# Bias folds and denominators of a fused graph layer, moved into four column tiles of 32

## The reference, cut to what matters

```python
xn = layernorm(x)
# graph part: a second layernorm with gain and bias, then attention over edges
x2 = layernorm(xn) * ln_g + ln_b
q, k, v = x2 @ Wq + bq, x2 @ Wk + bk, x2 @ Wv + bv
# softmax over the edges of a node of (q . k) * scale * edge weight, times v
gnn = xn + (values @ W1 + b1) @ W2 + b2
# mixer: linear attention
Q, K, V = elu(xn @ mWq + mbq) + 1, elu(xn @ mWk + mbk) + 1, xn @ mWv + mbv
kv = einsum('shd,she->hde', K, V)
z  = 1 / einsum('shd,hd->sh', Q, K.sum(0))        # the denominators
mix = einsum('shd,hde,sh->she', Q, kv, z) @ mWp + mbp
x = x + gnn + mix
x = x + ffn(layernorm(x))                          # digits of a one-hot code, elementwise
```

## Time and profile before

| what | value |
|---|---|
| median of three runs | 835.73 us |
| time of the profiled execution | 838.25 us |
| its span, first to last instruction | 836.1 us |
| mean granted TensorE clock | 0.974 |
| PE busy | 771.1 us, 92% |
| DVE, ACT, POOL busy | 67%, 43%, 47% |
| share of PE in the chain that ended last | 85% |

### The profile page before, as it was taken

One profiled execution on the slowest core, in us unless ns is written; L12 is line 12 of the kernel. 1 busy time (PEld: TensorE's weight loads), 2 busy tenths in 40 slices (PEclk: granted clock), 3 DMA queues, 4 the chain that ended last, 5 costly groups with the idle time before them and its releaser, 6 DMA issues.

```text
span 836.1 us, 13681 instructions
## 1 busy us (share of the span) xinstructions
PE 771.1 (92%) x4752; PEld 468.5 (56%) x4791; DVE 562.4 (67%) x1293; ACT 358.0 (43%) x834; POOL 393.0 (47%) x391
## 2 busy tenths in 40 slices
PE   1999998989999999969999999999999999999964
PEld 1564445544456444426666666666666876776742
DVE  4478584964232513358888888988888786786874
ACT  0321301022302122026666666666666764565562
POOL 1017787777777777777777777640000010010000
PEclk9989999999999999969999999999999999999987
DMA  7698959697474865005353535355341324324003
GB/s 226 155 377 294 342 196 333 218 368 255 145 252 118 301 220 205 3 5 205 105 203 107 204 107 191 116 172 198 112 192 67 133 94 152 107 89 145 32 1 123
DMA packets 69634, 143.64 MB, mean 172 GB/s; under 512 B 22187, under 2 KB 54251, under 8 KB 65599
## 3 DMA queue, kind: packets, MB, share of 16 engines
q1 hardware_dynamic: 47084, 119.42, 39.8%
q10 hardware_dynamic: 9136, 17.39, 6.3%
q0 software_dynamic: 13344, 5.92, 3.6%
HBM read 77.99 MB, written 64.80 MB: 171 GB/s over the span
## 4 chain that ended last, share of the span: by engine, by line
PE 85%; DVE 5%; DMA 4%; issue 2%; ACT 2%; ACTq 1%; another core or an unknown queue 1%; DVEq 0%
PE bank L898 17%; PE bank L1125 12%; PE bank L1093 12%; PE bank L892 12%; PE bank L1107 10%; PE bank L1098 6%; PE bank L1153 4%; PE bank L1131 2%; PE bank L1006 2%; DMA AR<-w_tab 1%; PE bank L881 1%; DMA AR<-in_L_gnn_b_dram 1%; PE bank L995 1%; PE bank L957 1%; DVE AR L1548 1%
## 5 line engine op out<-in xcount | busy, mean ns | idle before, releaser
L519 POOL DMA_INDIRECT w_tab<-pay,idx x330 | 338.9, 1027 | 153.5 <-issue 99.9
L770 ACT ACTIVATE AR<-AR,nmx 128x512 f32<-128x512 f32 (+1 forms) x160 | 106.6, 667 | 104.4 <-DVE nmx L1552 103.1
L1093 PE MATMUL bank<-KT,QT 64*128 64x512 f32 (+1 forms) x480 | 119.4, 575 | 8.1 <-issue 5.7
L1125 PE MATMUL bank<-AR,V 128*64 128x128 f32 (+1 forms) x1600 | 114.5, 281 | 0.0
L892 PE MATMUL bank<-AR 128*128 128x512 f32 (+1 forms) x288 | 106.6, 529 | 5.2 <-issue 1.8
L1548 DVE CUSTOM_DVE_ANT_0 AR<-bank,AR,MX 128x512 f32<-128x512 f32 (+1 forms) x106 | 100.9, 989 | 14.5 <-PE bank L1098 8.4
L898 PE MATMUL bank<-AR 128*128 128x512 f32 x240 | 107.1, 601 | 2.5 <-ACT AR L701 2.5
L592 POOL DMA_INDIRECT AR<-kv_rows,xd x10 | 10.9, 1090 | 207.2 <-PE bank L1125 185.0
L1125 PEld LDWEIGHTS bank<-AR,V 128*64 128x64 f32 (+1 forms) x1600 | 85.2, 137 | 20.6 <-issue 20.6
L892 PEld LDWEIGHTS bank<-AR 128*128 128x128 f32 x288 | 54.8, 193 | 52.3 <-issue 46.0
L779 ACT ACTIVATE AR<-bank 128x512 f32<-128x512 f32 (+1 forms) x120 | 66.6, 555 | 40.4 <-PE bank L1107 39.5
(11 more groups left out here) (259 smaller groups left out, 956.3 us busy)
## 6 DMA issues: line engine op xcount, KB each, us to landing
w_tab<-ztile SPq DMA_DIRECT2D x20, 2280.0 KB, 14.9
AR<-w_tab SPq DMA_DIRECT2D x20, 2048.0 KB
AR<-w_tab SPq DMA_DIRECT2D x10, 1344.0 KB
w_tab<-ztile SPq DMA_DIRECT2D x3, 1800.0 KB, 12.2
w_tab<-pay,idx POOLq DMA_INDIRECT x330
w_tab<-ztile SPq DMA_DIRECT2D x2, 1700.0 KB, 17.0
kv_rows<-AR ACTq DMA_DIRECT2D x9, 256.0 KB
kv_rows<-V ACTq DMA_DIRECT2D x9, 256.0 KB
```

Source lines behind the costliest of these rows:

```text
L519: pool.indirect_dma_start(out=w_tab, out_offset=bass.IndirectOffsetOnAxis(ap=idx[:, k, j:j + 1], axis=0), in_=pay[:, k % RING, j, :], in_o ...
L770: act.activation(ws[u % 3][hh][:, 0:n], ws[u % 3][hh][:, 0:n], ACT.Exp, bias=nmx[:, u % 4, hh:hh + 1], accum_out=DG[g][:, c, 2 * p + hh:2 ...
L1093: mm(bs[hh][:, 0:m], qs[hh], KT[64 * hh:64 * hh + 64, p, d0:d0 + m], start=True, stop=False)
L1125: last = mm(bank[4 + w % 2][64 * hh:64 * hh + 64, p * P:(p + 1) * P], v, PT[u % 2][hh][0:rws, i * P:(i + 1) * P], start=(i == 0), stop=(i ...
```

## The change

Four things are done another way. **Parts in column tiles.** `parts` writes the product of block k into partitions 32k to 32k+31 of a bank, with 32 equal columns of weights and no adding up, so that the four matmuls go to four column tiles of the array. It serves the query's and the key's bias (both now ahead of the first transposes) and b1 @ W2; the denominators do the same with 32 columns of `ksE`. **Sums.** A matrix `fourth` (128 x 8, made by DVE from the identity at the start) adds the four groups up afterwards: eight matmuls of one column for the two biases (`fold_sums`), one of 512 columns for b1 @ W2, and ten with eight columns in place of the ten transposes of `zt`. **Copies.** The parts have to be in SBUF for that: DVE copies the query's (`fold_parts`), ACT the key's and those of `ball`. **Order.** DVE normalises the first piece's rows ahead of the copy of the columns, and the row `ball` is finished after W1's transposes. The fold of the value stays as it is.

```diff
-PROJ += [("ball",)] + [("w1t", m) for m in range(KC)] + [("den", j) for j in range(3)] + [("kvt",)]
+PROJ += [("parts",)] + [("w1t", m) for m in range(KC)] + [("ball",)] + [("den", j) for j in range(3)] + [("kvt",)]
...
-        ksE = ar(17408, KC * H).rearrange("p (k h) -> p k h", k=KC)
-        dT = ar(17952, NP, H)
+        ksE = ar(17408, KC * 32).rearrange("p (k h) -> p k h", k=KC)
+        dT = ar(17952, NP)
...
             roots(0)
+            act.wait_ge(s_bp, 2)
+            act.activation(folds[1], bank[5][:, :], ACT.Copy).then_inc(s_fk, 1)
             gain_row(0)
...
+            r = PROJ_OF["parts",]
+            act.wait_ge(s_pr, r + 1)
+            act.activation(ball, bank[2 + r % 4][:, :], ACT.Copy).then_inc(s_pf[r % 4], 1)
...
+            def parts(b, c, w):
+                for k in range(KC):
+                    last = mm(b[32 * k:32 * k + 32, :], cols[:, c, k:k + 1].to_broadcast([P, 32]), w[:, k, :], start=True, stop=True)
+                return last
+            def fold_parts():
+                pe.wait_ge(s_cols, 1)
+                pe.wait_ge(s_w4[0], 16)
+                parts(bank[7], 1, sWq).then_inc(s_bp, 1)
+                pe.wait_ge(s_w4[1], 16)
+                parts(bank[5], 1, sWk).then_inc(s_bp, 1)
+            def fold_sums():
+                pe.wait_ge(s_fq, 1)
+                pe.wait_ge(s_fk, 1)
+                for i in range(2):
                     for m in range(KC):
-                        for k in range(KC):
-                            last = mm(bank[7][:, 4 * i + m:4 * i + m + 1], w[:, k, m * P:(m + 1) * P], cols[:, 1, k:k + 1], start=(k == 0), stop=(k == KC - 1))
+                        last = mm(bank[7][:, KC * i + m:KC * i + m + 1], folds[i][:, m * P:(m + 1) * P], fourth[:, 0:1], start=True, stop=True)
...
-            fold(0)
+            fold_parts()
             spread(0)
             transpose_x(0)
+            fold_sums()
...
-            b = proj(("ball",))
-            for k in range(KC):
-                last = mm(b[:, :], cols[:, 5, k:k + 1].to_broadcast([P, P]), sW2[:, k, :], start=(k == 0), stop=(k == KC - 1))
-            last.then_inc(s_pr, 1)
+            parts(proj(("parts",)), 5, sW2).then_inc(s_pr, 1)
...
+            b = proj(("ball",))
+            taken(pe, ("parts",))
+            mm(b[:, :], fourth[:, 0:1].to_broadcast([P, P]), ball, start=True, stop=True).then_inc(s_pr, 1)
...
-                    last = mm(b[0:H, 0:n * P], ksE[:, k, :], QM[:, k, t0 * P:(t0 + n) * P], start=(k == 0), stop=(k == KC - 1))
+                    last = mm(b[32 * k:32 * k + 32, 0:n * P], ksE[:, k, :], QM[:, k, t0 * P:(t0 + n) * P], start=True, stop=True)
...
-                        last = nc.tensor.transpose(b[:, t * H:(t + 1) * H], dT[:, t * P:(t + 1) * P], ident[0:H, 0:H])
+                        last = mm(b[:, t * H:(t + 1) * H], dT[:, t * P:(t + 1) * P], fourth[:, :], start=True, stop=True)
...
+            ch.link(v.tensor_reduce(fourth[:, :], ident[:, :].rearrange("p (k h) -> p h k", k=KC)[:, 0:H, :], AX.X, ALU.add))
             moments(0)
+            normed(0)
             dve.wait_ge(s_colp, 1)
             v.tensor_copy(cols[:, :, :].rearrange("p i k -> p (i k)"), bank[7][:, 32:32 + 6 * KC]).then_inc(s_cols, 1)
-            normed(0)
             dve.wait_ge(s_cols, 1)
+            fold_parts()
             take_x(0)
-            fold(0)
+            fold_sums()
...
-            fold(1)
             order_checks()
```

More of the change, by code:

```diff
@@ L181, in gps_layer @@
         nmx = sb("nmx", [P, 4, 2])
+        fourth = sb("fourth", [P, H])
         df = sb("df", [P, 2, H])
@@ L198, in gps_layer @@
         crow = ar(19520, P, 6 * KC)
+        folds = [ar(19520 + 512 * i, 512) for i in range(2)]
+        ball = ar(20488, 512)
         KM = [ar(13312 + 512 * i, 512) for i in range(2)]
@@ L327, in gps_layer @@
         s_bp = sem("biases_folded")
+        s_fq = sem("query_parts_copied")
+        s_fk = sem("key_parts_copied")
         s_be = sem("biases_ready")
@@ L728, in _ @@
                 act.wait_ge(s_pr, r + 1)
-                act.activation(dT[:, t0 * P:(t0 + n) * P], bank[2 + r % 4][0:H, 0:n * P], ACT.Copy).then_inc(s_pf[r % 4], 1)
+                act.activation(dT[:, t0 * P:(t0 + n) * P], bank[2 + r % 4][:, 0:n * P], ACT.Copy).then_inc(s_pf[r % 4], 1)
             r = PROJ_OF["kvt",]
@@ L868, in proj, with fold_row @@
                 return bank[2 + r % 4]
-            def fold(i):
-                pe.wait_ge(s_w4[i], 16)
-                if i == 0:
-                    pe.wait_ge(s_cols, 1)
-                w = (sWq, sWk, sWv)[i]
-                if i:
-                    pe.wait_ge(s_be, i)
-                if i < 2:
-                    for m in range(KC):
-                        for k in range(KC):
-                            last = mm(bank[7][:, 4 * i + m:4 * i + m + 1], w[:, k, m * P:(m + 1) * P], cols[:, 1, k:k + 1], start=(k == 0), stop=(k == KC - 1))
-                else:
-                    for k in range(KC):
-                        last = mm(bank[7][:, :], cols[:, 1, k:k + 1].to_broadcast([P, P]), w[:, k, :], start=(k == 0), stop=(k == KC - 1))
+            def parts(b, c, w):
[12 more added lines that the diff above has]
+                for i in range(2):
+                    for m in range(KC):
+                        last = mm(bank[7][:, KC * i + m:KC * i + m + 1], folds[i][:, m * P:(m + 1) * P], fourth[:, 0:1], start=True, stop=True)
+                last.then_inc(s_bp, 1)
+            def fold_row():
+                pe.wait_ge(s_w4[2], 16)
+                pe.wait_ge(s_be, 2)
+                for k in range(KC):
+                    last = mm(bank[7][:, :], cols[:, 1, k:k + 1].to_broadcast([P, P]), sWv[:, k, :], start=(k == 0), stop=(k == KC - 1))
                 last.then_inc(s_bp, 1)
@@ L920, in _ @@
                     transpose_x(j + 1)
-                if j == 0:
-                    fold(1)
                 qk("k", j, sWk, lambda k: x2T[j % 2][:, k, 0:n * P])
                 if j == 0:
-                    fold(2)
+                    fold_row()
                 for i in range(n):
@@ L1265, in take_x, with fold_parts, fold_sums, fold_row @@
                                            in1=r2B[:, t0 * P:(t0 + n) * P], op0=ALU.mult, op1=ALU.mult).then_inc(s_td, 1)
-            def fold(i):
-                dve.wait_ge(s_bp, i + 1)
-                if i == 0:
-                    ch.link(v.tensor_tensor(qbias[:, :], bank[7][:, 0:KC], cols[:, 2, :], ALU.add))
-                    v.tensor_scalar(qbias[:, :], qbias[:, :], SCALE, None, ALU.mult).then_inc(s_be, 1)
-                elif i == 1:
-                    v.tensor_tensor(kbias[:, :], bank[7][:, KC:2 * KC], cols[:, 3, :], ALU.add).then_inc(s_be, 1)
-                    dve.wait_ge(s_be, 2)
-                else:
-                    dve.wait_ge(s_row, 48)
-                    ch.link(v.tensor_tensor(bias_row[0][:, :], bank[7][:, :], bias_row[0][:, :], ALU.add))
+            def fold_parts():
+                dve.wait_ge(s_bp, 1)
+                v.tensor_copy(folds[0], bank[7][:, :]).then_inc(s_fq, 1)
+            def fold_sums():
+                dve.wait_ge(s_bp, 3)
+                ch.link(v.tensor_tensor(qbias[:, :], bank[7][:, 0:KC], cols[:, 2, :], ALU.add))
+                v.tensor_scalar(qbias[:, :], qbias[:, :], SCALE, None, ALU.mult).then_inc(s_be, 1)
+                v.tensor_tensor(kbias[:, :], bank[7][:, KC:2 * KC], cols[:, 3, :], ALU.add).then_inc(s_be, 1)
+                dve.wait_ge(s_be, 2)
+            def fold_row():
+                dve.wait_ge(s_bp, 4)
+                dve.wait_ge(s_row, 48)
+                ch.link(v.tensor_tensor(bias_row[0][:, :], bank[7][:, :], bias_row[0][:, :], ALU.add))
             def take_k(j, m):
```

## The result

| | before | changed |
|---|---|---|
| median, range | 837.93 us of 4 runs, 834.46 to 841.0 | 825.62 us of 4 runs, 822.7 to 826.84 |
| profiled execution, its span | 838.25, 836.1 | 826.6, 824.8 |
| mean granted clock | 0.974 | 0.978 |

The ratio of the two is 0.9838, 95% interval 0.9811 to 0.9865. By the medians it is 12.3 us and by the two spans 11.3, against the 9.0 of the forecast's sum. In a second comparison, on another chip, the changed kernel had a median of 826.33 (6 runs), the kernel before 837.24 (17 runs): ratio 0.9875, 0.9829 to 0.9921, and 10.9 us by the medians. The forecast's time and range hold, and the time by some luck: it was taken from 835.73, the median of three runs of the kernel before, and the fourth run moved that to 837.93. From there the forecast's 9.0 us would have given 828.9, 3.3 above what was measured.

A forecast was written before the change was run, and what follows sets the result against it. PE, holding 85% of the chain, was taken to bound the kernel. Second place 6.1 plus first place 2.9 gave 9.0 us off the 835.73 median: 826.8 us, range 821.5 to 832.5.

The forecast's parts named there:

- Second place: From 282.8 us on, `ball`, `den` and `zt` on PE ahead of attention: 6.1 us saved.
- The switches: PE enters and leaves the tiled form four times in the second place: 0.15 us each, 0.6 lost in all.
- rival 3: Clock falls behind the small matmuls of `zt`, costing up to 3.4 us: 830.2 us, 15%.
- Rivals 2 and 4: Tiles overlap only by twos: 829.8 us, 17%. Column tiles run one after another, slower: 839.1 us, 5%.
- 3.2 times for four tiles: Speed of `parts` and `den` at the skill's share of the ideal: 3.8 us not 3.1, total gain 0.7 smaller.
- First place: From 17.7 us on, query and key biases folded on PE at the start: 1.2 to 4.6 us saved, 2.9 taken.
- The gain is cut here: At DVE's marker check near 80 us, waiting for edge weights limits the first place's gain; keys some 8 us earlier.
- That load hangs on neither PE nor DVE: The edge weights' load on SP's queue, landing at 79.94 us, was taken not to depend on either engine.
- takes the first values at 80.97 as before: DVE, after the marker check, takes the first values at an unchanged time, with second queries from 83.7 us.
- rival 1: The cut at the edge weights does not happen; first place gives up to 8 us: 821.5 us, 10%.
- DVE now comes at 72.7, waits 7 us: DVE reaches the marker check at 72.7 us and waits 7 us for edge weights, where it waited 2.08.
- The rest of the program up to 282 us follows PE and ACT and moves with it: Between the second queries and the second place, the first place's 2.9 us gain is kept.

The follow-up runs named there:

- uncut_after2: Changed kernel with the marker check moved behind DVE's first four takes of values, second run: median 821.23 us, ratio 0.9806 to the kernel before.
- late_after: Changed kernel with ACT's loads of bias rows, last x and mixer query weights issued behind its key copies, marker check unmoved: 1192.6 us on a disturbed chip.
- late_uncut: Changed kernel with those ACT loads behind its key copies and the marker check behind the first four takes of values: median 809.48 us, ratio 0.9679 to the kernel before.
- held_after: Changed kernel with ACT's loads of bias rows, last x and mixer query weights held until the edges' rows landed: 1196.8 us on a disturbed chip.
- after2: The changed kernel unaltered, run again in the second comparison: median 826.33 us of 6 runs, ratio 0.9875 to the kernel before.
- mid_only2: Kernel before with the second place of the change alone, second run: median 832.28 us of 12 runs, ratio 0.9926 to the kernel before.
- mid_only: Kernel before with the second place of the change alone, first run, on a disturbed chip: 1193.8 us beside 1199.5 for the kernel before.

## Why the prediction held, and where it did not

**Second place, forecast 6.1: right.** 6.5 was measured, in each of the four undisturbed kernels that have it. *ball* 3.44 - 0.99 - 0.86 = 1.6 (forecast 1.7), *den* 8.69 - 2.29 = 6.4 (6.5), *zt* -1.4 (-1.5). The switches, for which I took 0.6, cost at most 0.4: 0.13 and 0.12 are lost in the tiled products, which the terms above already hold, and 0.15 in W1's transposes. No fall of the clock stands behind `zt` (1.00 from 302.6 to 313), so rival 3 is out. Rivals 2 and 4 are out by 3.8 times. So is my 3.2 times for four tiles. The Trainium skill, "TensorE: Matmul & The Clock Gate", section "Measured speedup vs the span model", gives 2.38 times for three column tiles and no figure for four; carrying its share of the ideal over was mine, and the trace does not agree with that.

**First place, forecast 2.9: its frame right, its number wrong.** "The gain is cut here" is shown by uncut_after2 and late_after. Two steps failed. The first is "That load hangs on neither PE nor DVE", and with it "takes the first values at 80.97 as before". The edge weights' load stands behind the edges' windows on SP's queue, and the change held that queue up: it was issued at 58.29 for 55.77 and landed at 82.4 for 79.9, so the values were first taken at 83.47 and the queries began at 86.3 rather than 83.7. SP's order did not change, as rival 1 says against itself, but ACT moved its own loads 3.2 us forward, into SP's window. "DVE now comes at 72.7, waits 7 us" failed too (79.05 and 3.39 us, since the rows came 6.8 us later; late_uncut, late_after and held_after bring them back to 41), but with no effect on the queries: in late_after DVE came at 72.4, and the queries at 88.2.

The second step is "The rest of the program up to 282 us follows PE and ACT and moves with it". It does not. The 2.1 us that were left at the second queries, and 1.0 at their end (they ran 1.1 us longer, at half clock for a start), did not last: in the profiled run the stores of keys and values were waited for 1.3 us longer (8.50 for 7.17), PE ran at half clock once more in the queries behind that wait (8.86 us where 7.17 stood) and longer behind the small matmuls (10.20 for 8.90), so that the parts began 4.1 us *later* than `ball`. On the chip of the second comparison after2 was 5.1 us ahead of mid_only2 at the second queries and 1.2 at the parts. So the first place gives little or nothing by then.

**Attention's start: not in the forecast, 6.4 us.** I had the row (0.87 in the stretch 355 to 361, in the earlier trace rows) and read it as a sign of how long a fall lasts. I did not ask why PE stood 5.74 us there, 3.1 of them with DVE's mask ready. It was the jump, a cost that no line of the diff touches and that is gone in 7 of 7 profiles with the change's code on PE. Some 3 of the 6.4 us are the jump itself and the rest the clock behind it, as the experiments above tell them apart. The Trainium skill, "Advanced Engine Details and Errata", section "Control Flow Timing", gives a compare-and-branch some 108 ns. The trace does not agree for this one: it has 0.36 to 3.85 us.

So the sum, 9.0 against 11.3 in the profiled pair, is near by luck, by two errors that offset one another: 2.9 forecast and -4.1 found, 0 forecast and 6.4 found. The remaining 2.6 (0.2, 0.9 and 1.5 us) go with a tile that came 0.4 us late and not 1.4, and with a higher clock at the end (0.86 to 0.87 for 0.83 in the last 45 us), which I did not follow further. Of the signs named ahead, `parts`, `den`, `zt` and the 6.5 to 7 us came; DVE's wait of 7 us and the queries at 83.7 did not; and the start of attention, which was to be at least 5 us earlier, is 5.7 earlier by PE's first product and only 2.6 by the first mask. What stays open: the first place's own time in undisturbed runs, what decides the jump's cost, what beside the six loads lengthens SP's window, and why late_uncut's stores are not waited for.

## What to carry to other kernels

When an engine gets ahead, list every transfer that it issues, and see on which transfer of another queue each one now falls: here six loads moved up by 3 us, and rows on another queue landed 7 us later; moving them to where their engine has nothing to do, together with the wait that was next in line, gave more (16.9 us) than the whole change (10.9 on that chip). Either alone gave less: 5.1 us for the wait, and for the loads no earlier queries at all. Do not take the landing of a load as fixed because its own queue's order is. Look at each idle stretch on the bound engine whose releaser had long been done, jumps included. And take a sum that comes out right for proven only when each of its terms has been found in the trace.

## What the runs showed of the hardware

- Four column tiles of 32 with 512 columns run at 3.8 times the rate of one after another (2.29 for 8.69 us); at each of three places beside a change between tiles and the full array 0.12 to 0.15 us more than the ideal were measured.
- A conditional jump on PE cost 0.36 to 0.46 us in eight profiles and 3.2 to 3.9 in six. The same kernel had 3.18 in one and 0.46 in another; 20 transposes added to code that is never reached went with 3.35 where 0.45 stood (one profile).
- One issue of a load on SP's queue took 18.3 to 19.9 us with six loads of ACT's queue issued some 9 us after its start, 13.7 to 13.9 with these six issued after its end, and 9.1 to 10.5 in the kernels with the old start; what makes the last difference is not shown.
- At the start PE's products took about twice their later time (eight parts 3.64 us, four 0.99 later) in a stretch where the granted clock reads 1.00.
- On the disturbed chips PE stood still, in mid_only for 77.5 us at a time, in code that it runs without a pause elsewhere.
